# Half of each expert's second product computed with the activations stationary, its bias added as a gated row

## The reference

```
scores = softmax(einsum('bsd,ed->bse', x, router_w))
gate_vals, sel_idx = top_k(swapaxes(scores, 1, 2), 257)
tokens = x[b_idx, sel_idx]
h = gelu(einsum('becd,edh->bech', tokens, w1) + b1)
y = einsum('bech,ehd->becd', h, w2) + b2
out = zeros_like(x).at[b_idx, sel_idx].add(y * gate_vals[..., None])
x = x + out
```

## Time and profile before

| | |
|---|---|
| time, median of 3 runs | 837.75 us (835.34 to 842.58) |
| span of the profiled execution | 832.3 us |
| lowest run less that span | 3.04 us |
| busy PE, PEld | 766.2 us, 627.0 us |
| busy DVE, ACT, POOL | 534.6 us, 396.6 us, 303.0 us |
| experts (612 us to the end) | 220.3 us of the span |

### The profile page before, as it was taken

The page is one execution under the profiler, slowest core; times in us unless marked ns, Lnnn a source line. Parts: engine busy times, 40 slices in busy tenths (PEclk is TensorE's granted clock), DMA queues, the critical chain, the costliest instruction groups (busy, mean ns, idle before and its releaser), DMA issues.

```text
span 832.3 us, 12982 instructions
## 1 busy us (share of the span) xinstructions
PE 766.2 (92%) x4971; PEld 627.0 (75%) x4971; DVE 534.6 (64%) x1148; ACT 396.6 (48%) x694; POOL 303.0 (36%) x275
## 2 busy tenths in 40 slices
PE   7899889999999999999999989984689999999996
PEld 7765546756656555579979888883689999999996
DVE  7777784576676684266454589985747755666551
ACT  3555443464455334564381345433035765557561
POOL 5511002100211023047371142334335767666673
PEclk9999999999999999999999999996899999999999
DMA  7000000000000100010021201120212445444532
GB/s 184 2 1 0 1 0 1 1 1 1 0 1 1 52 2 1 7 45 3 2 61 37 102 1 52 51 76 27 102 32 71 134 108 147 133 90 104 139 38 27
DMA packets 20359, 38.28 MB, mean 46 GB/s; under 512 B 4786, under 2 KB 15754, under 8 KB 17994
## 3 DMA queue, kind: packets, MB, share of 16 engines
q1 hardware_dynamic: 13641, 29.02, 10.7%
q0 software_dynamic: 6656, 8.43, 6.0%
HBM read 28.91 MB, written 8.40 MB: 45 GB/s over the span
## 4 chain that ended last, share of the span: by engine, by line
PE 60%; DVE 16%; ACT 4%; issue 3%; POOL 2%; DMA 0%; ACTq 0%; DVEq 0%
PE ps L464 19%; PE ps L1148 12%; PE ps L626 9%; PE ps L730 5%; PE ps L647 2%; PE ps L648 2%; PE ps L588 2%; DVE rep L1743 1%; DVE sm L1544 1%; DVE Pb L1548 1%; PE ps L1088 1%; PE ps L1076 1%; DVE sm L1553 1%; PE ps L563 1%; PE ps L798 1%
## 5 line engine op out<-in xcount | busy, mean ns | idle before, releaser
L626 PE MATMUL ps<-PT,VA 128*65 128x512 f32 (+1 forms) x288 | 147.5, 594 | 1.7 <-ACT PT L2035 1.3
L2035 ACT ACTIVATE PT<-ps 128x512 f32<-128x512 f32 x128 | 75.7, 592 | 63.4 <-PE ps L648 63.4
L1148 PE MATMUL ps<-he,wh 128*128 128x258 f32 x768 | 104.1, 288 | 0.0
L464 PE MATMUL ps<-GT,wh 128*128 128x258 f32 x768 | 96.4, 284 | 0.4 <-DVE GT L1841 0.4
L1148 PEld LDWEIGHTS ps<-he,wh 128*128 128x128 f32 x768 | 95.4, 189 | 0.4
L464 PEld LDWEIGHTS ps<-GT,wh 128*128 128x128 f32 x768 | 93.3, 189 | 0.6 <-issue 0.6
L2634 POOL DMA_INDIRECT out_dram<-ye,idx x40 | 64.1, 1603 | 22.6 <-DVE ye L1853 12.0
L1871 DVE TENSOR_TENSOR he<-het,he 128x516 fp32r<-128x516 f32 x64 | 44.6, 697 | 41.4 <-ACT he L1899 40.8
L2388 POOL TENSOR_TENSOR ssq<-ssq,half 128x8 f32<-128x8 f32 x16 | 26.1, 1638 | 122.6 <-DVE ssq L1269 122.6
L647 PE MATMUL ps<-QA,KA 128*128 128x512 f32 x144 | 68.5, 476 | 0.4 <-ACT QB L1899 0.4
L588 PE MATMUL ps<-KA,QA 128*128 128x368 f32 x192 | 59.7, 418 | 3.8 <-DVE x L1353 2.9
(11 more groups left out here) (286 smaller groups left out, 1556.0 us busy)
## 6 DMA issues: line engine op xcount, KB each, us to landing
wr<-in_w1e_dram SPq DMA_DIRECT2D x8, 1024.0 KB, 4.9
wr<-in_w2e_dram SPq DMA_DIRECT2D x8, 1024.0 KB, 4.8
x<-in_x_dram SPq DMA_DIRECT2D x4, 512.0 KB, 6.7
w<-in_w_dram SPq DMA_DIRECT2D x2, 1024.0 KB, 5.0
y_dram<-yr SPq DMA_DIRECT2D x3, 512.0 KB, 3.0
out_dram<-x SPq DMA_DIRECT2D x3, 512.0 KB, 4.1
gt<-y_dram,idx POOLq DMA_INDIRECT x40, 3.3
out_dram<-ye,idx POOLq DMA_INDIRECT x40, 3.9
```

The source lines that it names most:

```text
L464: op = pe.matmul(o, l, r, start=n == 0, stop=n == len(calls) - 1)
L626: pe.matmul(bank[6 + hf][0:65, :], VA[b][0:K, kt, h, :], PT[u % 4][0:K, :], start=kt == 0, stop=kt == 8).then_inc(p_pv, 1)
L1148: op = pe.matmul(bank[dc][:, 0:258], w2h[i][:, wc_], he[j][:, m, 258 * c:258 * c + 258], start=n == 0, stop=n == 23)
L2035: a.activation(PT[u % 4][0:K, :], bank[4 + u % 2][0:K, :], ACT.Exp, bias=0.0 if K == 128 else mcol[:, b:b + 1]).then_inc(a_exp, 1)
```

## The change

Groups 0 and 1 of the second product stay as they were. Groups 2 and 3 (the second half of the tokens) have their operands exchanged: 128 columns of `he` (one slot of tokens) are the stationary operand, and all 256 columns of a slice of `wh2` move. Group 2 then gives the finished rows of slot 2, group 3 those of slot 3, with tokens on the partitions. There are 24 matmuls in each group as before, of 256 columns where there were 258.

The bias is then no longer a value of the partition but a row. SP fetches it, copied to all partitions, into `b2r` (`fetch_b2`, 1 KB a partition). GpSimd multiplies it by the gates of slots 2 and 3 into `gb2` (`gated_row`), and DVE computes rows x gate + `gb2` from PSUM into `ye` in one instruction for each slot (`row_out`). The turning of slots 2 and 3 by PE, their rows in `yT`, two of ACT's four instructions on `yT` and the two multiplications of DVE are gone.

```diff
@@ tensor_program @@
                     op.then_inc(p_h, 1)
                     next(second, None)
-                    if ex and m == 0:
-                        pe.wait_ge(a_yT, 4 * ex)
-                        rows_out(ex - 1, 3, ((0, (2, 3)),))
...
                 for n_ in range(4):
-                    c, dc = divmod(n_, 2)
+                    dc = n_ % 2
                     clear(dc)
...
-                        wc_ = slice(256 * m + 128 * dc, 256 * m + 128 * dc + 128)
-                        op = pe.matmul(bank[dc][:, 0:258], w2h[i][:, wc_], he[j][:, m, 258 * c:258 * c + 258],
-                                       start=n == 0, stop=n == 23)
+                        if n_ < 2:
+                            wc_ = slice(256 * m + 128 * dc, 256 * m + 128 * dc + 128)
+                            op = pe.matmul(bank[dc][:, 0:258], w2h[i][:, wc_], he[j][:, m, 0:258], start=n == 0, stop=n == 23)
+                        else:
+                            c0 = COLS[n_][0]
+                            op = pe.matmul(bank[dc][:, 0:256], he[j][:, m, c0:c0 + 128], w2h[i][:, 256 * m:256 * m + 256],
+                                           start=n == 0, stop=n == 23)
...
                         if n_ == 2 and n == 11:
-                            pe.wait_ge(a_yT, 4 * ex + 2)
+                            pe.wait_ge(a_yT, 2 * ex + 2)
                             rows_out(ex, 0, ((6, (0, 1)), (7, (4,))))
                     op.then_inc(p_y, 1)
-                    busy[dc] = (a_yT, 4 * ex + n_ + 1)
+                    busy[dc] = (a_yT, 2 * ex + n_ + 1) if n_ < 2 else (v_ye, 5 * ex + n_ + 2)
                 drain(side_)
-            pe.wait_ge(a_yT, 4 * NE)
-            rows_out(NE - 1, 3, ((0, (2, 3)),))
@@ vector_program @@
+            def row_out(ex, s):
+
+                v.wait_ge(p_y, 16 + 4 * ex + s + 1)
+                v.wait_ge(g_con, 6 + ex + 1)
+                v.scalar_tensor_tensor(ye[ex % 2][:, s, :], bank[s - 2][:, 0:256], gate[:, ex, s:s + 1], gb2[ex % 2][:, s - 2, :],
+                                       ALU.mult, ALU.add).then_inc(v_ye, 1)
...
                 for m in range(8):
-                    if ex and m == 1:
-                        rows_out(ex - 1, ((0, (2, 3)),))
...
+                row_out(ex, 2)
                 drain(side_)
                 if ex + 1 < NE:
                     w2n, c = wh2[(ex + 1) % 2], slice(1024, 2048)
                     v.wait_ge(a_wh, 2 + 6 * ex + 6)
                     v.tensor_tensor(w2n[1][:, c], wr[1][:, c], f(w2n[0][:, c]), ALU.subtract).then_inc(v_wh, 1)
-            rows_out(NE - 1, ((0, (2, 3)),))
+                row_out(ex, 3)
@@ scalar_program @@
-                    c, dc = divmod(s, 2)
-                    a.wait_ge(p_y, 16 + 4 * ex + s + 1)
...
+                    if s < 2:
+                        a.wait_ge(p_y, 16 + 4 * ex + s + 1)
@@ gpsimd_program @@
+            def gated_row(ex):
+
+                g_.wait_ge(d_ln, 64 + 16 * (ex + 1))
+                if ex >= 2:
+                    g_.wait_ge(v_ye, 5 * (ex - 2) + 5)
+                g_.tensor_tensor(gb2[ex % 2][:, :, :], b2r[ex % 2][:, :].unsqueeze(1).to_broadcast([128, 2, D]),
+                                 gate[:, ex, 2:4].unsqueeze(2).to_broadcast([128, 2, D]), ALU.mult).then_inc(g_con, 1)
...
                 if ex:
                     scatter(ex - 1, 3)
                     scatter(ex - 1, 4)
+                gated_row(ex)
@@ sync_program @@
+            def fetch_b2(ex):
+                sp.dma_start(b2r[ex % 2][:, :], A["b2r"][ex].partition_broadcast(128)).then_inc(d_ln, 16)
...
                     fetch_w(ex + 2, 0)
+                    sp.wait_ge(g_con, 6 + ex + 1)
+                    fetch_b2(ex + 2)
```

More of the change, by code:

```diff
@@ L266, in build @@
         ye = [s4(f"ye{i}", [128, 5, D]) for i in range(2)]
-        yT = s4("yT", [128, 2, 516])
+        yT = s4("yT", [128, 2, 258])
+        b2r = [s4(f"b2r{i}", [128, D]) for i in range(2)]
+        gb2 = [s4(f"gb2{i}", [128, 2, D]) for i in range(2)]
         assert s4.at <= sc_at
@@ L1844, in rows_out @@
             def rows_out(ex, banks):
-                if ex >= 2 and banks[0][0] == 6:
+                if ex >= 2:
                     v.wait_ge(d_scat, 80 * (ex - 1))
@@ L1849, in rows_out @@
                 for n, (b_, ss_) in enumerate(banks):
-                    v.wait_ge(p_yT, 3 * ex + {6: 1, 7: 2, 0: 3}[b_])
+                    v.wait_ge(p_yT, 2 * ex + {6: 1, 7: 2}[b_])
                     for i, s in enumerate(ss_):
@@ L2351, in scalar_program @@
                                 copy(w2n[:, c], wr[1][:, c]).then_inc(a_wh, 1)
-                    c, dc = divmod(s, 2)
-                    a.wait_ge(p_y, 16 + 4 * ex + s + 1)
[L2354 to L2357, removed]
+                    if s < 2:
+                        a.wait_ge(p_y, 16 + 4 * ex + s + 1)
+                        if ex and s == 0:
+                            a.wait_ge(p_yT, 2 * ex)
+                        a.activation(yT[:, s, :], bank[s][:, 0:258], ACT.Identity, bias=b2e[:, ex, s:s + 1]).then_inc(a_yT, 1)
                     next(side_, None)
@@ L2759, in sync_program @@
             sp.wait_ge(p_rl, 5)
+            fetch_b2(0)
+            fetch_b2(1)
             for j in range(2):
@@ L2821 @@
         "b1e": I["L1_ffn_b1"].reshape(NE, 8, 128).transpose(2, 0, 1),
+        "b2r": I["L1_ffn_b2"],
         "b2e": I["L1_ffn_b2"].reshape(NE, 2, 128).transpose(2, 0, 1),
```

## The result

The changed kernel takes 832.57 us (median of 7 runs, 831.18 to 834.9) where the kernel before takes 838.28 (7 runs): a ratio of 0.9942 with a 95% interval of 0.9921 to 0.9963. In a second session the same kernel gave 0.9965 (0.9944 to 0.9985). The profiled execution took 831.18 us with a span of 829.1, against a span of 832.3 before.

What follows compares the result with a forecast made beforehand. PE, busy in all 26.42 us of a passage between experts, was taken as the bound. Gains of 3.1 (turning), 0.2 (exchanged operands) and 0.4 (tail) made 3.7 us: 837.75 becomes 834.0 us, range 830.0 to 838.5.

Steps and rivals of the forecast that it cites:

- the three signs by which it would be wrong: PE waits for ACT or DVE inside an expert; L1151's pace differs from L730's; the last scatter waits for DVE.
- The turning: Start of experts 1 to 7: PE saves four turnings of 0.11 us, 0.44 us in each of seven passages, 3.1 us.
- Rival 1: First product: ACT sets the pace and PE waits for its banks, so the gain is given back; 837.1 us, chance 0.07.
- The exchanged operands: Groups 2 and 3, 348 matmuls of 256 instead of 258 columns: 0 to 0.3 us gained, 0.2 us taken.
- Rival 3: Groups 2 and 3: the exchanged matmuls are slower, each 10 ns costing 3.5 us, the whole gain; 837.5 us, chance 0.05.
- GpSimd's product: New bias-gate product on GpSimd in each expert: costs nothing, covered by idle times while POOL's lateness stays below about 3 us.
- Its duration: GpSimd's new product takes 1.3 us, between 1.0 and 1.56; L1894 then takes about 1.6 us in every passage.
- DVE's moved rows: Rows of slots 2 and 3, moved earlier on DVE, cost nothing, with 0.6 us to spare before the first he.
- Expert 0 and SP: SP's bias fetch costs nothing; POOL and DVE lateness in expert 0 taken as nothing, up to 0.5 us kept for the range.
- The tail: End of the kernel: most of the saving is hidden behind GpSimd's scatters, so 0.4 us gained instead of some 3.
- Rival 4: Tail: the scatters aren't in the way, so the end gives 3.1 us instead of 0.4; 831.3 us, chance 0.03.
- Rival 2: Expert passages: a long GpSimd product delays DVE's first he, reaching PE from 3.0 us; at 5 us, 848 us; chance 0.05.

Runs made afterwards that it cites:

- e1_turn_back: Changed kernel with four unread turning matmuls put back on PE behind the first 12 matmuls of experts 1 to 7: passage 26.20 us against 25.78, stage 216.24 against 213.45.
- e6_last_early: Changed kernel with GpSimd's bias-gate product for expert 7 made right behind that for expert 6: expert 7 to first scatter 20.03 us against 20.97, stage 212.41 against 213.45.
- e7_product_by_act: Changed kernel with the bias-gate product made by ACT, none on GpSimd: passage 25.78 us as before, stage 212.39 against 213.45.
- e4_product_twice: Changed kernel with GpSimd's bias-gate product made twice in a row: passage 25.78 us as before, expert 7 to first scatter 22.59 against 20.97, stage 214.89 against 213.45.
- e8_turn_sooner: Changed kernel with the turning of slots 0, 1 and 4 six matmuls sooner, in the last expert alone: stage 212.76 us against 213.45.
- e5_product_thrice: Changed kernel with GpSimd's bias-gate product made three times: passage 25.78 us as before, expert 7 to first scatter 20.03 against 20.97, stage 212.47 against 213.45.
- e10_256_columns: Changed kernel with groups 0 and 1 also moving 256 columns, slot 4 left out of the second product: passage 25.65 us against 25.78, stage 212.44 against 213.45.
- e9_together: Changed kernel with the edits of e6_last_early and e8_turn_sooner plus repeated stationary operands in groups 0 and 1: 831.30 us, ratio 0.9938 to the kernel before; stage 211.55.

## Why the prediction was right

It forecast 834.0 us and a gain of 3.7 us; measured were 832.57 and, by the profile, 3.2 us of span, 3.0 of them in the stage that was changed. That the time came so close is in part luck. The forecast added 5.45 us from span to median, from three runs; behind the change the median lies 3.5 us above the span (832.57 - 829.1), which brings the time 2.0 us down, while the span is 0.5 us longer than the 828.6 forecast. The medians' own difference, 5.7 us, is 2.0 above the forecast gain. Two of the three signs by which it would be wrong also came: PE waits for DVE inside expert 7, and L1151 has another pace than L730. The last scatter doesn't wait for DVE. By its own terms:

- **The turning, 3.1 us.** Right. The six whole passages give back 157.22 - 154.66 = 2.56 us in e1_turn_back. The seventh turning lies in expert 7, where it lengthened the stretch by only 0.20, part of it falling into PE's wait there (DVE's held instruction took 2.34 us in that run instead of 2.60). It was PE's time, and nothing in its place became late in the passages. Rival 1 fell: the 96 matmuls of each first product are one row of 11.62 to 11.67 us in the six passages, without a wait for ACT.
- **The exchanged operands, 0.2 us.** Right in mechanism, mis-sized: the forecast allowed up to 0.8 ns a matmul and took 0.2 us. The passages show 0.51 - 0.42 = 0.09 us each, 1.9 ns a matmul and about 0.65 us in all, expert 0 with it. The step is the price taken from L730, the same form, read as 119.8 ns; L1151 has 36 in 4.26 us, 118.3. Why L730's rows read higher is open. Rival 3, slower matmuls, fell with it.
- **GpSimd's product, nothing.** Right for experts 0 to 6, wrong for expert 7. The step that failed is "covered by these idle times": the idle times read were those of a passage, and the last turn of GpSimd's loop has another order around it. There is no low part of `wh2` and no gather after it; five scatters stand ahead and DVE's `he` beside it. It cost 0.9 us once (e6_last_early, e7_product_by_act). The forecast used exactly this collision, between L2651 and L1887 in the earlier trace rows, for the passages and did not ask where else the new instruction would meet a DVE instruction with two operands in SBUF.
- **Its duration.** The forecast took 1.3 us; by starts it is 1.01, and 1.04 by the record of a repeated one (e4_product_twice), as the lower bound from L2444 said. So L2666 is done before L1894, and this kept its 1.20 us everywhere but in expert 6, where it took 4.00 us before and 3.06 after; 1.6 us "in every passage" was wrong, without effect.
- **DVE's moved rows, nothing.** Right in cost. The order was told wrong: row_out of slot 2 stands behind the index reductions, at 668.45, and not in DVE's wait before them.
- **Expert 0 and SP, nothing.** Expert 0, which has no turning before it, became 0.11 us shorter, about the 0.09 of the exchanged matmuls, so the half microsecond kept for it wasn't needed.
- **The tail, 0.4 us.** Right: 0.26, and its cause, the scatters, is shown by e8_turn_sooner. Rival 4, 3.1 us, fell.
- **Rival 2, GpSimd becomes the bound.** The point from which it decides was put at 3.0 us of product. With 3.83 us (e5_product_thrice) no passage grew. At which duration it starts is open.

The stage adds up so: 3.10 us in the six passages, 0.11 in expert 0, 0.47 in expert 7 without its new wait (20.50 - 20.03 of e6_last_early), less 0.94 for that wait, and 0.26 in the tail, together 3.00. Against the 3.7 forecast, 0.9 us were not foreseen in expert 7 and some 0.25 are missing in the turning and the tail; some 0.45 more came from the exchanged operands.

## What to carry to other kernels

Where one engine is busy without a gap, an instruction taken from it is worth its own time: here 0.44 us read as the distance between the two rows around it, and 0.42 when it was put back. At the end of a kernel the same removal is worth only what the next chain leaves: count the serial instructions behind it first. And read the first and last turn of a loop apart from the middle ones; work that fits into an idle time in every middle turn can lie beside something else in the last; here moving it by one turn cost nothing (e6_last_early).

## What the hardware showed that I had not expected

- **A DVE instruction was held up by a GpSimd one whose record starts later.** In the last expert DVE's `he`, both inputs in SBUF, starts at 807.01 and GpSimd's product at 807.40 by the records, yet DVE's takes 2.60 us instead of 0.70, and GpSimd's its usual 1.64. The Trainium skill (SBUF — State Buffer, section "Who interferes with whom") calls the port that the two share an exclusive lock and says that the order of issue decides which of them blocks. By the records' starts it would be GpSimd; the trace has DVE blocked. But DVE's head start bought it nothing: it ended about 0.57 us after the end of the product's record whether it had started 0.13 us before that record (e1_turn_back), 0.39 (after) or 0.62 (e4_product_twice). So either the records of GpSimd don't give the true order or DVE's instruction was stopped under way; no run here decides. What is shown is that DVE paid, and that its 2.60 us go when the product does. A sum that counts on DVE starting first, by the records, should not.
- **Two moving columns cost more than their share.** From 258 to 256 columns a matmul became 2.1 to 2.6 ns shorter (e10_256_columns), at a granted clock of 1.00, where the share of two columns in 2.90/24 = 120.8 ns is 0.9. Why is open.
- **A stationary operand loaded twice in succession** saves nothing that shows to 0.01 us in a long row: 48 matmuls in 5.77 us with 16 repeats (e9_together) and without (e6_last_early).
